# An attention and feed-forward kernel: the square of the value weights gets a place of its own in ScalarE's order, and most other events get new places

## What is computed

```python
y = x * rsqrt(mean(x * x, -1) + 1e-6) * rms_w
y = einsum('bsm,cm->bsc', y, w_in)               # 32 q heads, 8 k and 8 v heads, 64 wide
q, k = rope(q), rope(k)
qk = einsum('bghsd,bgxpd->bghsp', q, k) * 64 ** -0.5      # 4 q heads share one k, v (a group)
attn = softmax(where(causal, qk, -inf))
o = einsum('bghsp,bgxpd->bghsd', attn, v)
x = layernorm(x + (x + einsum('bsc,mc->bsm', o, w_out)))
x_q = ternary(x, 0.33, 0.5);  w = ternary(weight, 0.2, 0.6) + rram_variation
x = layernorm(x + einsum('bsd,od->bso', x_q, w))
```

## Time and profile before

| | |
|---|---|
| median of the runs shown | 1450.53 us (1447.55 to 1450.67) |
| profiled execution | 1448.91 us |
| its span, first to last instruction | 1447.0 us |
| mean granted TensorE clock | 0.975 |
| PE, DVE, ACT, POOL busy | 1355.5, 1139.6, 1093.1, 878.0 us |
| instructions | 25215 |

### The profile page before, as it was taken

The page is one execution under the profiler, slowest core; times in us unless marked ns, Lnnn a source line. Parts: engine busy times, 40 slices in busy tenths (PEclk is TensorE's granted clock), DMA queues, the critical chain, the costliest instruction groups (busy, mean ns, idle before and its releaser), DMA issues.

```text
span 1447.0 us, 25215 instructions
## 1 busy us (share of the span) xinstructions
PE 1355.5 (94%) x7328; PEld 1011.7 (70%) x7328; DVE 1139.6 (79%) x3047; ACT 1093.1 (76%) x2301; POOL 878.0 (61%) x872
## 2 busy tenths in 40 slices
PE   5789899999999999999999999999999999997896
PEld 3667676777777777776777777776777677774574
DVE  4778777886797788877797788877798787975896
ACT  4668778786787788787787788777787778885674
POOL 1447567485656666386546667386556667369766
PEclk9799999999999999999999999999999999998999
DMA  5002111211101111111101111121111111011012
GB/s 203 19 19 59 42 31 29 54 32 40 35 23 48 49 32 32 39 44 41 34 27 48 48 29 33 26 59 42 30 28 47 49 30 34 26 45 45 27 45 84
DMA packets 45161, 61.79 MB, mean 43 GB/s; under 512 B 10464, under 2 KB 27104, under 8 KB 45024
## 3 DMA queue, kind: packets, MB, share of 16 engines
q1 hardware_dynamic: 45024, 60.20, 14.3%
HBM read 34.74 MB, written 4.46 MB: 27 GB/s over the span
## 4 chain that ended last, share of the span: by engine, by line
PE 79%; ACT 6%; DVE 6%; POOL 4%; issue 3%; DMA 1%; SPq 1%; POOLq 0%; DVEq 0%; ACTq 0%
PE x L1150 18%; PE s L1138 18%; PE t L1192 15%; PE x L1176 11%; PE ot L1107 8%; PE ot L1109 7%; ACT prob L815 2%; DVE prob L989 1%; ACT prob_hi L783 1%; DVE prob_lo L1073 1%; DMA raw<-L_ffn_rram_variation 1%; PE x L1166 1%; DVE stats L890 1%; PE x L1094 1%; POOL raw L521 1%
## 5 line engine op out<-in xcount | busy, mean ns | idle before, releaser
L1073 DVE SCALAR_TENSOR_TENSOR prob_lo<-t,prob_hi 128x512 f16<-128x512 f32 x576 | 394.8, 687 | 84.0 <-ACT prob_hi L783 79.3
L783 ACT ACTIVATE prob_hi<-t 128x512 f16<-128x512 f32 x576 | 339.2, 592 | 152.6 <-PE t L1192 147.4
L1138 PE MATMUL s<-k_t,q_t 128*128 128x512 f32 (+3 forms) x1536 | 413.1, 373 | 25.6 <-POOL q_t L733 7.5
L815 ACT ACTIVATE prob<-prob,neg_max 128x896 f32<-128x896 f32 (+7 forms) x512 | 393.1, 769 | 30.3 <-DVE neg_max L989 28.9
L1192 PEld LDWEIGHTS t<-ident,prob 128*128 128x128 f32 x2304 | 290.0, 142 | 105.4 <-ACT prob L815 6.1
L1192 PE MATMUL t<-ident,prob 128*128 128x128 f32 x2304 | 349.2, 274 | 2.8 <-ACT prob L815 2.7
L989 DVE CUSTOM_DVE_ANT_0 prob<-s,mask 128x512 f32<-128x512 f32 (+3 forms) x512 | 292.8, 586 | 70.1 <-PE s L1138 40.9
L1138 PEld LDWEIGHTS s<-k_t,q_t 128*128 128x128 f32 x1536 | 246.5, 193 | 62.7 <-DVE neg_max L989 12.5
L756 POOL TENSOR_TENSOR o_lo<-o_raw,o_hi 128x256 fp32r<-128x256 f32 x128 | 94.4, 737 | 258.6 <-ACT o_hi L883 258.2
L1107 PE MATMUL ot<-prob_hi,v_sb 128*128 128x512 f16 x576 | 225.6, 392 | 2.3 <-DVE o_raw L1055 1.5
L1109 PE MATMUL ot<-prob_lo,v_sb 128*128 128x512 f16 x576 | 220.5, 383 | 6.9 <-DVE prob_lo L1073 6.7
(11 more groups left out here) (97 smaller groups left out, 2019.8 us busy)
## 6 DMA issues: line engine op xcount, KB each, us to landing
swapped<-flat SPq DMA_DIRECT2D x320, 64.0 KB, 2.0
spread<-recip_rows SPq DMA_DIRECT2D x128, 128.0 KB
recip_rows<-turned SPq DMA_DIRECT2D x512, 0.5 KB
raw<-L_attn_w_in SPq DMA_DIRECT2D x8, 768.0 KB, 7.6
raw<-L_attn_w_out SPq DMA_DIRECT2D x8, 512.0 KB, 3.7
out<-acc SPq DMA_DIRECT2D x16, 256.0 KB, 2.0
acc<-L_attn_x SPq DMA_DIRECT2D x3, 1024.0 KB, 10.6
acc<-L_attn_x SPq DMA_DIRECT2D x4, 256.0 KB, 3.6
```

What stands on the lines that cost most here:

```text
L783: act.activation(prob_hi[:, u % 2, :], t_ps[u % 2][:, :], ACT.Copy, scale=P_SCALE).then_inc(prob_hi_done, 1)
L815: act.activation(row, row, ACT.Exp, bias=neg_max[:, kk % 4, h:h + 1], scale=-1.0, accum_out=total[:, kk % 4, h:h + 1]).then_inc(ex_done, 1)
L1073: dve.scalar_tensor_tensor(out=prob_lo[:, u % 2, :], in0=t_ps[u % 2][:, :], scalar=P_SCALE, in1=prob_hi[:, u % 2, :], op0=ALU.mult, op1=AL ...
L1138: mm = pe.matmul(s_ps[:, off:off + cols], q_t[:, h, s * P:(s + 1) * P], k_t[:, part, keys:keys + cols], start=(part == 0), stop=(part == 1))
```

## The change

The event `nv` is split. ACT's square becomes an event `nq` of its own, and both get places from a new entry NORM_V. ACT's part of `w`, which overwrites win_hi, now waits in all passes but the first for the last projection of the group that reads it, pj111. All other tables, FIRST included, get new numbers; of them only those that the text below speaks of are shown.

```diff
@@ body_plan
-        put(at_pass["W_IN"][-1] + 10, ("nv",))
+        put(at_pass["NORM_V"][0], ("nq",))
+        put(at_pass["NORM_V"][1], ("nv",))
@@ ACT, event w
                             if plan is first:
                                 act.wait_ge(rms_in, 16)
+                            else:
+                                wait_x_full(act, plan, g, ("pj", 1, 1, 1))
                             act.activation(win_hi[:, e[1], :], win_raw[:, e[1], :], ACT.Copy, scale=rms[:, e[1]:e[1] + 1]
@@ ACT, the square
-                        elif e[0] == "nv":
+                        elif e[0] == "nq":
 
                             wait(act, win_hi_done, g, 4, 8)
@@ FIRST
-    ('xn', 0), ('sq', 0), ('xn', 1), ('xn', 2), ('norm', 0), ('w', 0), ('xn', 3), ('norm', 1), ('w', 1), ('w', 2),
-    ('norm', 2), ('norm', 3), ('w', 3), ('nv',), ('xn', 4), ('xn', 5), ('sq', 1), ('pj', 2, 0, 2), ('sw', 2, 0, 2),
+    ('sq', 0), ('xn', 0), ('xn', 1), ('w', 0), ('w', 1), ('xn', 2), ('norm', 0), ('norm', 1), ('xn', 3), ('w', 2),
+    ('w', 3), ('sw', 2, 0, 2), ('nq',), ('norm', 2), ('norm', 3), ('nv',), ('consts',), ('sq', 1), ('xn', 4),
...
@@ OPENING
-    W_IN=(296, 296, 300, 300),
+    W_IN=(259, 262, 278, 284),
+    NORM_V=(295, 302),
@@ OPENING, PROJECT: pj, sw, ro, hl of the chunks 112, 110 and 111
-        (((190, 190, 218, 259), (221, 224, 236, 276), (266, 287, 309, 314)), 260),
+         (((189, 194, 211, 258), (222, 205, 237, 272), (267, 267, 310, 317)), 259),
@@ MIDDLE
-    W_IN=(255, 260, 287, 294),
+    W_IN=(254, 263, 277, 287),
+    NORM_V=(293, 301),
@@ MIDDLE, PROJECT, the same chunks
-        (((203, 205, 226, 232), (218, 240, 258, 291), (251, 258, 280, 324)), 245),
+         (((201, 202, 207, 235), (216, 241, 236, 299), (251, 247, 298, 318)), 245),
@@ FINAL
-    FFN_IN=(
-        (254, 314), (322, 334), (344, 366), (374, 388)
-    ),
+    FFN_IN=((255, 318), (321, 341), (335, 365), (378, 396)),
```

More of the change, by code:

```diff
@@ L88 @@
 FIRST = (
[8 rows of a table removed]
-)
-OPENING = dict(
-    SCORES=(
[14 rows of a table removed]
-    ),
-    PROJECT=(
[5 rows of a table removed]
-    ),
-    SQUARES=(0, 3),
[L124 to L127, removed]
-    LOAD=213,
-    W_IN=(296, 296, 300, 300),
-    OUTPUT=(
[3 rows of a table removed]
-    ))
-MIDDLE = dict(
-    SCORES=(
[14 rows of a table removed]
-    ),
-    PROJECT=(
[4 rows of a table removed]
-    ),
-    W_OUT=(51, 51),
-    LOAD=177,
-    W_IN=(255, 260, 287, 294),
-    OUTPUT=(
[3 rows of a table removed]
-    ))
-FINAL = dict(
-    SCORES=(
[13 rows of a table removed]
-    ),
-    PROJECT=(
-        (((18, 34, 59, 145), (46, 56, 139, 192), (156, 176, 177, 202)), 150),
-        (((208, 212, 238, 239), (221, 237, 277, 313), (277, 282, 310, 325)), 263)
-    ),
-    W_OUT=(29, 30),
-    FFN_IN=(
-        (254, 314), (322, 334), (344, 366), (374, 388)
-    ),
-    OUTPUT=(
[3 rows of a table removed]
-    ),
-    LAYER=(
[6 rows of a table removed]
-    ))
[9 rows of a table added]
@@ new lines @@
+OPENING = dict(
+    SCORES=(((0, 1, 5, 14), (5, 15, 19, 22), 43, 74), ((17, 34, 39, 43), (23, 35, 44, 46), 65, 101),
[12 rows of a table added]
+    PROJECT=((((1, 8, 19, 26), (16, 8, 30, 42), (33, 29, 53, 54)), 26),
[4 rows of a table added]
+    SQUARES=(0, 3),
+    NORMS=((11, 23), (24, 27), (29, 37), (41, 44), (45, 52), (61, 95), (96, 157), (158, 167)),
+    W_OUT=(29, 34),
+    LOAD=197,
+    W_IN=(259, 262, 278, 284),
+    NORM_V=(295, 302),
+    OUTPUT=((130, 186, 117, 293), (4, 4, 21, 70), (30, 51, 55, 63), (37, 57, 59, 81), (32, 56, 62, 90), (28, 66, 74, 92),
+         (44, 30, 68, 87), (31, 34, 44, 69), (6, 13, 20, 30), (17, 18, 25, 46), (14, 38, 51, 62), (38, 47, 48, 59),
+         (28, 38, 71, 90), (36, 40, 63, 77), (28, 38, 67, 92), (22, 22, 38, 62), (180, 76, 32, -53)))
@@ new lines @@
+MIDDLE = dict(
+    SCORES=(((0, 0, 0, 3), (1, 2, 8, 11), 45, 92), ((8, 16, 21, 29), (18, 24, 27, 42), 51, 108),
[12 rows of a table added]
+    PROJECT=((((53, 81, 96, 143), (117, 124, 152, 175), (154, 197, 189, 194)), 152),
[3 rows of a table added]
+    W_OUT=(45, 49),
+    LOAD=176,
+    W_IN=(254, 263, 277, 287),
+    NORM_V=(293, 301),
+    OUTPUT=((15, 16, 26, 41), (22, 33, 44, 73), (35, 44, 58, 70), (39, 47, 56, 87), (30, 32, 65, 92), (46, 56, 58, 93),
+         (31, 36, 74, 107), (29, 50, 50, 84), (13, 24, 32, 43), (24, 27, 33, 44), (25, 28, 35, 61), (23, 39, 40, 77),
+         (21, 33, 48, 68), (26, 27, 29, 49), (40, 45, 53, 86), (14, 12, 34, 61), (-178, 143, 88, 51)))
@@ new lines @@
+FINAL = dict(
+    SCORES=(((2, 11, 11, 18), (4, 6, 15, 16), 34, 36), ((23, 25, 26, 29), (36, 41, 41, 41), 48, 52),
[10 rows of a table added]
+    PROJECT=((((18, 48, 102, 143), (42, 76, 155, 185), (167, 197, 180, 197)), 153),
+         (((202, 207, 205, 233), (222, 235, 281, 312), (276, 267, 293, 326)), 261)),
+    W_OUT=(29, 36),
+    FFN_IN=((255, 318), (321, 341), (335, 365), (378, 396)),
+    OUTPUT=((22, 9, 25, 33), (23, 22, 26, 52), (23, 26, 38, 60), (38, 40, 61, 65), (30, 47, 58, 77), (22, 32, 62, 83),
+         (20, 20, 31, 77), (12, 20, 53, 82), (6, 4, 28, 39), (27, 27, 42, 59), (39, 38, 70, 90), (51, 53, 70, 90),
+         (57, 56, 64, 106), (44, 29, 77, 105), (55, 55, 64, 88), (23, 12, 35, 57), (23, 30, 49, 69)),
+    LAYER=((358, 396, 404, 412, 417, 418, 469), (386, 397, 413, 429, 444, 443, 480), (389, 399, 439, 446, 450, 456, 490),
[5 rows of a table added]
```

## The result

The changed kernel takes 1457.97 us (median of six runs, 1454.65 to 1460.17) against 1450.02 of the kernel before in six runs beside it: ratio 1.0057, 95% interval 1.0039 to 1.0074. It is slower by 8 us, where 27 us of gain were forecast (1423, range 1411 to 1438). The profiled execution took 1460.1 us, its span is 1458.2, its mean granted clock 0.983 (before 0.975).

The account below looks back on a forecast made before the run. PE (TensorE) was taken as the bound, its idle time and low clock to be won: 1448.9 - 18.5 (stops) - 11.9 (clock) + 4.8 (DVE) - 2.1 (opening) = 1421.2, on the median's scale 1423 us; range 1411 to 1438.

Parts of the forecast that it names:

- What is late next in a middle pass: Slots 31 to 39 of middle passes: DVE falls short, costing PE 0.8 us a pass in small waits, +4.8 us.
- The other places: FIRST, the opening's first slots and FINAL: moves taken as 0, with 5 us allowed to either side for opening and final.
- The stops and the clock: Six middle-pass stops of PE for the square, 18.5 us, and half-clock stretches behind them, 11.9 us, go.
- rival (a): Middle passes, slots 35 to 39: PE's waits add up and the clock still falls; 1434.9 us, chance 0.13.
- DVE's term: Slots 35 to 39 of middle passes: small PE waits for DVE's prob_lo and neg_max, 0.8 us a pass.
- v_scale: Slot 37: DVE waits 1 to 2.5 us for POOL's v_scale, but PE's work covers it; 0, range 0 to 1.5 a pass.
- The opening: Opening pass: PE's waits of 2.6 us go, ACT's new wait for pj111 costs 0.5; net -2.1 us.
- Final pass and tail: Final pass: POOL's order around PE's 5.2 us wait for q_t stays; 0 taken, 5 us allowed either side.
- (d): Middle passes: DVE's missing lead and its v_scale wait gather in one stop, the clock falls behind it; 1460 us, chance 0.08.
- (b): Middle passes: ACT, with prob_hi, casts and exps behind transposes 37, takes the square's place, 1.5 us a pass; 1432, chance 0.14.
- (c): New order better everywhere: DVE keeps up and 0.9 us of middle-pass idle time goes too; 1412.8 us, chance 0.13.
- (e): Middle passes: the square waits for w3's cast, ACT gets to both late, the stop stays; 1450.5 us, chance 0.04.

Follow-up runs that it names:

- e9: The changed kernel with rs12, rs14 and rs16 of the middle table back at their old steps: 1429.31 us, ratio 0.9853.
- e12: The changed kernel, tables untouched, with each spread issued as two transfers of 64 partitions instead of one: 1419.19 us, ratio 0.9787.
- e4: The changed kernel with the square put back directly ahead of the norm matmuls: 1489.1 us, ratio 1.0261.
- e1: The kernel before, its old order kept, with only the square split off and placed earlier: 1437.9 us, ratio 0.9919.
- e6: The changed kernel with only rs14 of the middle table back at its old step, 403 instead of 414: 1449.46 us, ratio 0.9986.
- e8: The kernel before with the square split off and, in middle passes, only the new places of slots 27 to 41, rs12 at its old step: 1425.61 us, ratio 0.9825.

## Why the prediction was wrong

**The step that failed** is a term put at nothing without a reason: the rest of the middle pass. "What is late next in a middle pass" follows every event of slots 31 to 39; for the other 63 slots it names only a possible gain of 0.9 us a pass, and "The other places" speaks of FIRST, the opening and the final pass alone. Of the SP queue it looked at load_wout and at no `rs`. Six `rs` stand later there by more than two steps; three of them, later by 18, 11 and 26 steps, cost 28.7 us (e9) of the 35 between forecast and result. Their distances could be read from the tables: from rs12 to on12 the lead shrank from 4.0 to 1.5 slots, from rs14 to on14 from 3.0 to 1.5, from rs16 to on16 from 7.0 to 2.0 (on16 itself stands 17 steps earlier). But the tables alone do not tell which move costs: rs03 went from 4.0 slots ahead of on03 to 0.5 behind it and rs05 from 3.0 to 0.5, and POOL waits for neither, since it gets to on03 12.6 us and to on05 18.9 us behind their issue. What counts is that time, read from the trace. The trace of before showed that even the old lead was short: its spread went out at 673.77 and POOL used it at 679.92, 6.2 us later. The changed kernel's chain has the price of the transfer:

```profile
676.67 5.43 DMA spread<-recip_rows
```

In the kernel before, where no second spread ran beside it, the semaphore's updates show that it landed 4.4 us behind its issue: the old place had 1.7 us to spare, and rs12 moved by more than two slots. An event on SP has no busy time, which is why no table of busy engines shows it; and e12 with e9 shows that the length of the transfer and the place of the event cost together: either one mended alone takes the loss of the middle passes away (964.4 and 965.5 us).

**The stops and the clock, -30.4.** In size right, in part by luck: e4 shows 31.1, made up otherwise. But the reason given, the square's place alone, was wrong; `acc` ended the same stop (e1), and the gain came with the moves around it. On the clock rival (a) did not occur: the middle passes keep 1.00 although PE waits seven times, up to 1.3 us, in the one shown, and once 1.7 in another. The Trainium skill, "TensorE: Matmul & The Clock Gate", section "A second HAM failure mode: psum-queue depth-cycling", tells of a clock that falls again and again through frequent brief idling; the middle passes of this trace, with 4.5 us of short waits in 165, do not show it. It was a near thing: in e6 the clock fell to 0.50 in two middle passes behind a single stop of 1.5 us.

**DVE's term, +0.8 a pass.** Right. In the waits of the third middle pass PE waits 1.1 us for prob_lo in the changed kernel, and in e9, without the late spreads, 0.8 in two waits, at slots 36 and 38.

**v_scale, 0.** Right for the cost, not for the wait. DVE waits 0.73 us where it waited 0.66, less than the 1 to 2.5 that I estimated, and PE does not wait for it:

```profile
659.97 0.31 DVE L1004 TENSOR_SCALAR v_twice<-v_scale 64x1 f32<-64x1 f32 x2 [0.73 <-POOL v_scale L673]
```

**The opening, -2.1.** Wrong in sign for the pass: 194.5 against 193.1, though the prologue ahead of it is 2.5 shorter. Up to its norm matmuls the opening is 1.1 us shorter than before (114.6 and 115.7), behind them 2.5 longer. Two things were mis-sized. One is the wait on pj111, put at 0.5 within 0 to 2.8. In the changed kernel ACT waits 2.77 us there, and PE stops for 2.44:

```profile
147.84 0.61 ACT L799 ACTIVATE win_hi<-raw,rms 128x384 fp32r<-128x384 f32 x1 [2.77 <-PE x L1127]
150.42 0.39 PE L1086 MATMUL ot<-prob_lo,v_sb 128*128 128x512 f16 x1 [2.44 <-DVE prob_lo L1050]
157.81 0.58 PE L1135 MATMUL x<-ones,squares 128*128 128x2 f32 x4 [1.01 <-ACT squares L804]
```

The prediction priced what lies ahead of w0 on ACT, hl112's casts; they were long done, and ACT stood idle. What counted lay behind it: two casts, o_hi and an exp go first after 147.84, and prob_hi(33) only at 149.77. The two old waits of the earlier trace rows, 1.83 and 0.75, which the prediction took as gone, are now 2.44 and 1.01. No run leaves out the added wait in this order, so its part is read from these rows and not tested. The other is the clock, for which the forecast had no term here; behind the two stops it falls:

```profile
160.00:163.40 3.40, 3.40 (x8) 2.17 (x9) 2.33 (x7) 1.43 (x4) 1.50 (x3) 0.50 0.28 98
```

PE is busy throughout, so this costs 1.7 us. In e12 the first stop is 1.79 us, the clock stays at 1.00 there, and the opening takes 189.7; PE's wait for POOL's rotation in its first slots, 2.9 us and new in the changed kernel, is 0.8.

**Final pass and tail, 0.** The final pass is 188.2 (187.0), the tail behind it 37.7 us against 35.5. Together +3.3, inside the 5 allowed. In e12 the same final table takes 182.5, so the length of the spreads was a part of it. In the tail the clock is at 0.50 for 3.4 us from 1426.4 on with PE busy, 1.7 us that the kernel before does not have at this place; why it falls there stays open.

**The rivals.** The time is that of (d), 1460, but none of its mechanism occurred: no long stop for v_scale, no fall of the clock in a middle pass. (b), (c) and (e) did not occur either. The sum for the part that was counted holds: e8, which makes just that part in the middle passes, measured 1425.6 against the 1423 of the forecast (1425 without the 2.1 of the opening, which e8 leaves as it was), with passes of 160.4 in the mean against "about 160".

## What to carry to other kernels

When a change renumbers a hand-written order, list for each pair of dependent events the distance before and after, DMA issues first. Turn the distance into time with the trace, from the issue to the use, and look at those whose time falls to the length of the transfer; then ask whether the transfer can be made shorter before asking who may be moved. An engine's idle share does not say whether it may be late: follow what is queued behind the waiting instruction, link by link, to PE. Before a stop is given a price, read the rows of matmuls and of weight loads both; where they name different enders, removing one leaves the other.
